# Maxima of the next pair, placed by the columns that layer 1's attention streams

## The reference

```
x = x + conv_attention(group_norm(x))     # layer 0: 6 heads of 16, all 1024 keys, relative positions
t = t + causal_attention(layer_norm(t))   # layer 1: 6 heads of 16, keys up to the query's own
t = t + experts(layer_norm(t))            # 4 experts, 2 chosen per position, GELU
```

## Time and profile before

| | us |
|---|---|
| median of three runs | 2108.75 |
| profiled execution, span from first to last instruction | 2107.2 |
| busy: PE / DVE / ACT in that span | 1847.2 / 1248.2 / 1119.8 |
| layer 1's call, fifth of eight: pair 0 / pair 1 | 19.88 / 26.22 |
| the same call, pair 2, tile rows 0 to 6 | 19.32 |

### The profile page before, as it was taken

One profiled execution on the slowest core, in us unless ns is written; L12 is line 12 of the kernel. 1 busy time (PEld: TensorE's weight loads), 2 busy tenths in 40 slices (PEclk: granted clock), 3 DMA queues, 4 the chain that ended last, 5 costly groups with the idle time before them and its releaser, 6 DMA issues.

```text
span 2107.2 us, 25342 instructions
## 1 busy us (share of the span) xinstructions
PE 1847.2 (88%) x9408; PEld 742.6 (35%) x9408; DVE 1248.2 (59%) x2508; ACT 1119.8 (53%) x1423; POOL 144.7 (7%) x69
## 2 busy tenths in 40 slices
PE   2697589998899988998899988999889988999858
PEld 1132233343234433343333432344333433334323
DVE  5671676546764667636765467636676466744631
ACT  2256345674456744675456744567345745555433
POOL 3000002000020000200020000200002000200000
PEclk7599599999999999999999999999999999999979
DMA  6416400354016320263003440163202630002100
GB/s 139 58 35 110 75 12 19 86 66 83 11 30 116 68 39 18 51 101 68 21 19 86 66 83 11 30 116 70 37 19 51 101 68 15 17 11 59 27 11 8
DMA packets 55699, 110.98 MB, mean 53 GB/s; under 512 B 17686, under 2 KB 18903, under 8 KB 54040
## 3 DMA queue, kind: packets, MB, share of 16 engines
q1 hardware_dynamic: 54040, 109.06, 27.5%
q10 hardware_dynamic: 1536, 0.30, 0.1%
HBM read 61.82 MB, written 34.60 MB: 46 GB/s over the span
## 4 chain that ended last, share of the span: by engine, by line
PE 68%; DVE 18%; ACT 5%; DMA 4%; issue 3%; SPq 1%; POOL 1%; ACTq 0%; DVEq 0%; POOLq 0%
PE psOM L645 16%; PE psS L591 12%; PE psT L620 8%; DVE mx L1279 8%; PE psT L621 7%; PE psT L755 6%; PE psS L769 4%; PE psT L623 4%; DVE mrow L1381 3%; PE psT L541 3%; DVE qb L1408 2%; DVE x L1390 1%; PE psT L550 1%; DMA qr<-negb 1%; PE psT L800 1%
## 5 line engine op out<-in xcount | busy, mean ns | idle before, releaser
L1006 ACT ACTIVATE probs<-psT 128x1024 f32<-128x1024 f32 (+7 forms) x768 | 622.7, 837 | 524.3 <-PE psT L621 258.2
L1279 DVE TENSOR_REDUCE mx<-psS 128x1 f32<-128x512 f32 (+3 forms) x1152 | 704.9, 643 | 286.2 <-PE psS L591 217.2
L621 PE MATMUL psT<-qb,kb 97*128 97x512 f32 x768 | 415.6, 585 | 0.0
L645 PE MATMUL psOM<-probs,v 128*32 128x512 f32 (+3 forms) x2688 | 383.3, 558 | 11.6 <-ACT probs L1006 11.6
L591 PE MATMUL psS<-ka,qa 128*128 128x512 bf16 x768 | 298.8, 400 | 38.9 <-DVE mx L1279 19.8
L620 PE MATMUL psT<-qa,ka 128*128 128x512 bf16 x768 | 296.8, 386 | 11.8 <-DVE resid L1268 5.1
L755 PE MATMUL psT<-xf,w1s 97*128 97x512 f32 x384 | 187.8, 623 | 2.1 <-DVE mrow L1381 1.8
L623 PE MATMUL psT<-qr,kr 97*128 97x512 bf16 (+3 forms) x576 | 184.2, 349 | 4.3 <-DMA qr<-negb 3.3
L1408 DVE TENSOR_TENSOR qb<-psOM,qa 32x768 fp32r<-32x768 f32 x128 | 121.8, 952 | 101.6 <-ACT qa L1046 99.7
L769 PE MATMUL psS<-probs,w2s 128*96 128x512 f32 x384 | 180.7, 596 | 0.8 <-ACT att L1071 0.8
L591 PEld LDWEIGHTS psS<-ka,qa 128*128 128x128 bf16 x768 | 71.5, 97 | 308.8 <-DVE mx L1279 244.3
(11 more groups left out here) (146 smaller groups left out, 1651.3 us busy)
## 6 DMA issues: line engine op xcount, KB each, us to landing
scr<-split SPq DMA_DIRECT2D x32, 576.0 KB, 4.4
scr<-qb SPq DMA_DIRECT2D x16, 768.0 KB, 6.8
qr<-scr SPq DMA_DIRECT2D x48, 192.0 KB, 6.5
au<-ot SPq DMA_DIRECT2D x192, 32.0 KB, 2.0
lb<-ot SPq DMA_DIRECT2D x192, 32.0 KB, 2.0
qr<-scr SPq DMA_DIRECT2D x48, 128.0 KB, 4.4
kr<-scr SPq DMA_DIRECT2D x48, 128.0 KB, 7.3
qa<-scr SPq DMA_DIRECT2D x32, 128.0 KB, 3.7
```

Of the source, the lines that this page charges most:

```text
L621: last = mm(o[:, a:b], kb[:, h, ks], qb[:, h, a:b], start=False, stop=True)
L645: last = mm(psO[j:j + 2 * HD, a - c * HALF:HALF], v[:, kt, 2 * p + hh, :], probs[:, (2 * kt + hh) % 4, a:(c + 1) * HALF], start=kt == 0, s ...
L1006: A(probs[:, n % 4, q0:T], psT[:, t_slot(ts, m), q0:T], ACT.Exp).then_inc(t_free, 1)
L1279: V.reduce_max(mx[layer][:, p % 2, (h % 2) * NT + t, kc:kc + 1], psS[:, s_bank(st, fill), 0:max_cols(layer, t, kc)], AX).then_inc(s_free, 1)
```

## The change

In layer 1's call the maxima are no longer spread evenly over the thirty points of a pair. `pace1` gives each maximum a cost (150 plus its columns) and each point a weight: the columns of the products that stand before it, where the values' count is four times their columns. Maximum n is sent at the first point at which the share of the columns streamed covers the costs up to n. All eight tile rows of pairs 0 and 1 are used, and the first six of pair 2. A pair's own 24 maxima must still be out by tile row 5 of the pair before. Layer 0's call keeps the old rule. DVE's order is written from the same table: group_stats stands behind the first 24 reductions as before, group_var behind 13 more (6 before), group_norm behind 16 more (16 before).

Maxima sent in tile rows 0 to 7, where there is a lead:

| pair | before | after |
|---|---|---|
| 0 | 3 3 3 3 3 3 0 0 | 2 5 5 4 4 4 2 2 |
| 1 | 5 5 6 5 5 6 0 0 | 3 5 4 4 3 3 2 2 |
| 2 | 4 4 4 4 4 4 0 0 | 2 4 4 3 4 3 0 0 |

```
-LEAD_EARLY = 8
+MAX_BASE = 150
...
+def max_cost(steps):
+    return [MAX_BASE + max_cols(*step) for step in steps]
+
+def products1(kt):
+    q0 = kt * P
+    half = [max(0, (c + 1) * HALF - max(q0, c * HALF)) for c in range(NC)]
+    half = [n + P * (n > 0 and q0 >= c * HALF) for c, n in enumerate(half)]
+    return half + half + [4 * min(HALF, T - (kt - 1) * P) if kt else 0]
+
+def pace1(lead):
+    ends, total = [], 0
+    own = max_cost((1, t, kc) for _, t, kc in MAX_STEPS["attn1"])
+    own[:LEAD] = [0] * LEAD
+    costs = own + max_cost((0, t, kc) for _, t, kc in MAX_STEPS["lead"]) * lead
...
+    stretch = [sum(sum(products1(kt)) for kt in range(a, b)) for a, b in ((0, NT - 2), (NT - 2, NT))]
+    whole = PAIRS * sum(stretch) - stretch[1]
...
+        due = ends[min((p + 1) * PER_PAIR[1], len(ends)) - 1] if p + 1 < PAIRS else total
+        marks.append(max(due, total * (p * sum(stretch) + stretch[0]) / whole))
...
+                while sent < len(ends) and ends[sent] <= share + 1:
+                    sent += 1
+                out[p, kt, i] = sent
...
                     def between():
+                        if layer == 1:
+                            until = pace[(p, *divmod(points[0], 5))]
+                            for stage, fill in every[behind[0]:until]:
+                                if stage == "lead" and fill == 0:
+                                    pe.wait_ge(ab_in, upto("ab_in", it, "lead", 0))
+                                max_scores(it, stage, fill)
+                            behind[0] = until
                         points[0] += 1
...
             def attention1(it):
-                per = PER_PAIR[1]
-                maxima(it, "attn1", range(per))
+                pace = pace1(next_lead(it))
...
                 if next_layer0(it):
+                    until(0, PER_PAIR[1])
                     group_stats(it, "gn")
-                    maxima(it, "attn1", range(per, per + 6))
+                    until(PER_PAIR[1], pace[1, 0, 4])
                     group_var(it, "gn")
-                    maxima(it, "attn1", range(per + 6, per + 22))
+                    until(pace[1, 0, 4], pace[1, 5, 0])
                     group_norm(it, "gn")
-                    maxima(it, "attn1", range(per + 22, 2 * per))
+                    until(pace[1, 5, 0], pace[PAIRS - 1, NT - 1, 4])
```

More of the change, by code:

```diff
@@ L77, in seq @@
             for w in text.split()]
+def max_cost(steps):
[10 more added lines that the diff above has]
+    costs = own + max_cost((0, t, kc) for _, t, kc in MAX_STEPS["lead"]) * lead
+    for n in costs:
+        total += n
+        ends.append(total)
+    stretch = [sum(sum(products1(kt)) for kt in range(a, b)) for a, b in ((0, NT - 2), (NT - 2, NT))]
+    whole = PAIRS * sum(stretch) - stretch[1]
+    out, done, sent = {}, 0, LEAD
+    marks = [0]
+    for p in range(PAIRS):
+        due = ends[min((p + 1) * PER_PAIR[1], len(ends)) - 1] if p + 1 < PAIRS else total
+        marks.append(max(due, total * (p * sum(stretch) + stretch[0]) / whole))
+    for p in range(PAIRS):
+        own = 0 if p == 0 else stretch[1]
+        at = 0
+        for kt in range(NT):
+            for i, n in enumerate(products1(kt)):
+                at += n
+                if kt < NT - 2:
+                    share = marks[p] + (marks[p + 1] - marks[p]) * (own + at) / (own + stretch[0])
+                else:
+                    after = at - stretch[0]
+                    share = marks[p + 1]
+                    if p + 1 < PAIRS:
+                        share += (marks[p + 2] - marks[p + 1]) * after / (stretch[1] + stretch[0])
+                while sent < len(ends) and ends[sent] <= share + 1:
+                    sent += 1
+                out[p, kt, i] = sent
+    assert sent == len(ends), (sent, len(ends))
+    for p in range(PAIRS - 1):
+        assert out[p, NT - 3, 4] >= (p + 1) * PER_PAIR[1]
+    return out
 MIX = seq("gate gates u0 u1 R0 d0 H0 L0 H1 L1 v0 u2 d1 v1 ln den R1 u3 d2 u4 H2 L2 u5 res H3 d3 nrm L3 u6 d4 d5 tr R2 H4 L4 q0 q1 lev V0 "
@@ L650, in attention @@
                 lead = layer == 1 and next_lead(it)
+                pace = pace1(lead) if layer else {}
+                every = [("attn1", f) for f in range(len(MAX_STEPS["attn1"]))] + [("lead", f) for f in range(len(MAX_STEPS["lead"]))] * lead
+                behind = [LEAD]
                 if layer == 1:
@@ L657, in attention @@
                     next_q = layer == 0 and p == 1 and next_layer0(it)
[L658 to L662, removed]
+                    ahead = [(st, f) for f in range(p * n, (p + 1) * n)] if p + 1 < PAIRS else []
                     points, sent = [0], [0]
                     def between():
-                        points[0] += 1
[L668 to L673, removed]
+                        if layer == 1:
[5 more added lines that the diff above has]
+                            behind[0] = until
+                        points[0] += 1
+                        if layer == 0:
+                            until = min(len(ahead), len(ahead) * points[0] // (5 * (NT - 2)))
+                            for stage, fill in ahead[sent[0]:until]:
+                                max_scores(it, stage, fill)
+                            sent[0] = until
                     if layer == 0:
@@ L1438, in attention1, with until @@
             def attention1(it):
-                per = PER_PAIR[1]
-                maxima(it, "attn1", range(per))
+                pace = pace1(next_lead(it))
+                own = len(MAX_STEPS["attn1"])
+                def until(a, b):
+                    maxima(it, "attn1", range(min(a, own), min(b, own)))
+                    maxima(it, "lead", range(max(a - own, 0), max(b - own, 0)))
                 if next_layer0(it):
+                    until(0, PER_PAIR[1])
                     group_stats(it, "gn")
-                    maxima(it, "attn1", range(per, per + 6))
+                    until(PER_PAIR[1], pace[1, 0, 4])
                     group_var(it, "gn")
-                    maxima(it, "attn1", range(per + 6, per + 22))
+                    until(pace[1, 0, 4], pace[1, 5, 0])
                     group_norm(it, "gn")
-                    maxima(it, "attn1", range(per + 22, 2 * per))
+                    until(pace[1, 5, 0], pace[PAIRS - 1, NT - 1, 4])
                 else:
-                    maxima(it, "attn1", range(per, 2 * per))
-                if next_lead(it):
-                    maxima(it, "lead", range(len(MAX_STEPS["lead"])))
+                    until(0, pace[PAIRS - 1, NT - 1, 4])
             def attention0(it):
```

## The result

The changed kernel takes 2120.1 us, median of seven runs (2114.0 to 2126.0), where the kernel before took 2108.5 beside it (seven runs, 2105.8 to 2113.1). The ratio is 1.0055, with an interval of 1.0036 to 1.0074: slower, by some 12 us.

A forecast was written before the change was run, and what follows sets the result against it. PE sets the time, and layer 1's attention changes through PE's waits for DVE. Terms sum to +1.7 us per call, +11 over eight calls, plus 3 for the clock: 2121.2 by the profile, 2122 as a run; range 2104 to 2134.

The forecast's parts named there:

- The placement alone: Layer 1's maxima moved between pairs: pair 0 +4.8 us per call, pair 1 -3.3, pair 2 -1.1.
- the norm: Group norm in pair 1 moves to tile row 5, with fewer maxima around: 0.7 us of wait remains, -0.75 per call.
- rival 2: Faster: maxima cost 0.62 us each where DVE is overfull, 0.26 where it has slack; 2091; chance 0.13.
- Its own sign: Test for the faster case: a tile row of pair 0 with four or five maxima stays under 2.7 us.
- The statistics: Pair 0: maximum 26 needs 24's reduction, which stands behind the group statistics on DVE; PE waits, +2.0 us per call.
- the walk: Step-by-step timing of PE and DVE on two banks; PE, free since 1.6 us, sends maximum 26 at 3.6.
- The third of a group waits: Pair 0: the third maximum of each group of three waits about 0.75 us (0.7 as sign) for the first's reduction.
- The clock: Falls to 0.50 behind pair 0's new waits, costing about 1.0 us in every second of six calls: +3.
- Rival 3: The clock falls in each of six calls for two tile rows at 0.8 us: +9.6 for +3, 2129; chance 0.18.
- Rival 1: Pair 0 takes its ten maxima at about 0.37 us each, +3.7 for +4.8, without clock falls: 2112; chance 0.23.
- upper price: The clock falling at the new wait in each of six calls, +9.6 us in place of +3: 2129.

The follow-up runs named there:

- Statistics late: The changed kernel with group_stats behind 32 reductions, at the end of pair 0's tile row 6, instead of 24: 2108.2 us, ratio 1.0010 to the kernel before.
- two at most: The changed kernel with at most two maxima sent at one point, the others at the next: 2118.6 us, ratio 1.0063 to the kernel before.
- the fillers: The changed kernel with 24 unread 128-column products on PE before maximum 26 in the six calls with group norm: 2111.4 us, ratio 1.0020 to the kernel before.

## Why the prediction was right

The sign and the mechanism came out, and so did the sizes but for one. That the time agrees within 2 us (2122 forecast, 2120.1 measured) is in part luck: the clock cost more than forecast in the profiled execution, and the rest, put at nothing, took less. Step by step, for that execution, where the eight calls grew by 21.8:

- **The placement alone.** Forecast: +4.8, -3.3, -1.1 and, for the norm, -0.75, so -0.35 in each of six calls, and +0.9 for the last two, -1.2 in all. "Statistics late" shows +2.0 in the calls, of which five times 0.55 are statistics in pair 1's row 0; that leaves -0.8, nothing within the 2 or 3 us that tile rows 0 and 1 vary by. Single terms are sharper: pair 1 of the seventh call, without group norm, is 21.42 for 24.73, -3.31; pair 2 -1.25; pair 0 without the statistics 24.9 for 19.8 (means of six calls), +5.1. The norm still costs 0.56 in pair 1 (21.98 for 21.42), where 0.7 was forecast. That ten maxima in pair 0 cost as much as ten fewer elsewhere give back, or more, was the core of the forecast, and it holds (5.1 against 4.6): rival 2, which had full pace where DVE is overfull, would need pair 0 near 22.5. Its own sign, a tile row of pair 0 with four or five maxima under 2.7 us, is missing: rows 2 to 5 take 3.93, 2.74, 3.46 and 3.12 without the statistics.
- **The statistics.** Forecast +2.0 per call, with a wait of 2 at maximum 26. Maximum 26 was to go 3.6 after 23; it went 3.54 after (1281.63 to 1285.17), and PE was free a little later than in the walk. The wait is 1.74, and row 5 is longer by 5.01 - 3.13 = 1.9, in the first six calls only. Six times 1.9 is 11.3 for the forecast's 12.
- **The third of a group waits** 0.67, forecast 0.7. But "two at most" shows that this wait is no cost of the group: taken away there, it comes back a point later.
- **The clock** is the term that was mis-sized. Forecast: a fall of 1.0 in every second call, 3 in all. Measured: the falls came in four of six calls and cost 10.9, from 28.3 to 30.4 for pair 0 against 26.5, so 2 to 4 each. A fall lasted 6.83 to 10.24 us and slowed tile rows 5 to 7, in the second call by 1.6, 1.3 and 0.4 (6.63 for 5.02, 3.14 for 1.85, 2.66 for 2.23); I had counted hardly more than one tile row, at 0.8. Rival 3, with 1.6 in each of six calls, had the sum (9.6) nearer, with too many calls and too small a price.
- **What I had left out** gave it back: the rest was 5.1 lower in the changed kernel's profiled execution, with two falls of the clock within the mix for before's four. So 21.8 - 5.1 = 16.7 by the spans, above the forecast's 14, while the medians differ by 11.6. In the median run there were probably fewer falls than in the profiled one, which took 5.6 more. The mean granted clock, on record for every run, fits: 0.935 in the profiled run, 0.940 in the median one, 0.942 in the fastest. Which falls are missing it doesn't show, since only profiled runs show the clock by stretch. So what the falls behind the wait cost in a typical run stays open: the ratios with and without the fillers, 1.0055 and 1.0020, are 7 us apart, and that contains the rest's difference.

Rival 1 falls with pair 0 at 24.9 without the statistics: +5.1 over before's mean is nearer to the forecast's 4.8 than to 3.7.

Still open: what makes the clock fall behind the same wait in one call and not in the next, and within the mix in one image and one kernel and not in another.

## What to carry to other kernels

Work that an engine does on the side, in an order that is fixed, belongs where nobody who matters waits for what stands behind it: in the changed kernel, moving two such jobs to the end of a tile row won 23 us of the calls (529.8 to 506.7, some 11 of them from the clock, in the profiled executions), and the better spread of the maxima, with the jobs out of the way, 10 (500.6 to 490.6). A cost that is convex in each row calls for equal counts per row, read from the rows' measured times, and columns streamed were no measure of how much room a row has here, where the limit is two buffers and another engine's pace. When a table moves instructions, look at what is fixed relative to it, for a job that stood in a gap yesterday stands in a crowd today.

## What the runs showed of the hardware

A wait of PE of 1.74 us with 0.67 shortly ahead of it brought a granted clock of 0.50 (1.2 GHz) for 6.83 to 10.24 us in four calls, beginning within the wait in two and 1.1 and 1.7 us behind it in the other two, and none in the last two, with the same instructions around it. Twenty-four unread products in the wait kept it at 1.00 in all six calls of one execution, and the tile row took no longer for them. The Trainium skill, "TensorE: Matmul & The Clock Gate", section "Part 1: The HAM clock gate", has the throttled state as the default that activity releases; the fillers agree with it. The two calls without a fall show that the wait alone does not decide, so the fall at each call that the prediction drew from that rule for its upper price did not come. The same section calls the number of slow products at a kernel's start run-variable, by the phase in which the monitor meets the kernel. That the same holds here, call by call, would fit the four falls of six and the differing rest; no run here controls it.

With the fall the price is two to three times the wait's own: the side job on DVE cost 1.9 us where the clock held and 4 to 6 where it did not.
